# Sum of squares from VectorE to ScalarE, state cast from ScalarE to VectorE, in an 8-core scan and feed-forward layer

## The chip, the cores and the metric

The program runs on the 8 cores of one Trainium2 chip. Each core takes half of one of four sequences; no core waits for another. The metric is the device time of the slowest core in microseconds (us). Before the change it is 3581.18 us, the median of three runs (3579.0 to 3582.77).

## The reference

```python
xn = layernorm(x)                                   # x: 4 x 4096 x 2048, f32
xp = xn @ W_in.T
dt = softplus(xp @ W_dt.T + b_dt)                   # 32 heads
a  = exp(-exp(log_A) * dt)                          # per head and channel
ys[t] = a[t] * ys[t-1] + xp[t]                      # along the sequence
attn = ys @ W_out.T
ffn  = ((silu(xn @ w_gate * s_gate) * (xn @ w_up * s_up)) @ w_down) * s_down
out  = x + attn + ffn
```

`w_gate`, `w_up` and `w_down` are int8, with 8192 inner columns.

## The kernel before, in words

A core works on 2048 output rows and on 256 rows ahead of them, from which the scan takes its start. That makes 18 tiles of 128 rows of `x`. Semaphores are placed by hand; each engine runs its instructions in the order in which the program text emits them.

**Preamble (`emit_wc_step`, 16 steps).** The product of `W_dt` and `W_in` is built: a load of `winN` through GpSimd's queue, 16 small matmuls into `psdtl`, and a copy out by ScalarE (L231). Between these steps the normalization of the first ten tiles is started and of eight of them ended.

**Normalization of a tile.** `emit_ln_front` issues the load of the tile `xtb` on ScalarE's queue (L253) and lets VectorE wait for it; VectorE forms the sum (L259), the sum of squares (L260) and four results of one column (L264 to L271). `emit_ln_back` of that tile comes one to three fronts later: ScalarE makes the scale and the shift (L281 to L287) and the normalized tile `xnb` (L291); SyncE writes it to `xn_scr` (L297). There are three `xtb`, so three loads can be under way. The front of tile i waits for the normalized tile i-3.

**Transposes (`emit_tr`, five chunks).** SyncE waits for all writes of `xn_scr` that were issued, and then issues 16 transposing loads into `xnT` (L314). `emit_dtl` makes the step sizes from a chunk: matmuls L327, ScalarE's softplus (L334 to L343), VectorE's sum and split.

**Two passes over 16 column blocks (`emit_m1_et`).** The first pass covers chunks 0 and 1, the second chunks 2 to 4. A block has two or three small products that spread the step size over channels (L399, L402), ScalarE's exponential `ab` (L407), 32 or 48 matmuls of 512 or 256 columns into `ps_xp` (L421), ScalarE's copy `xpsb` (L436), VectorE's scan into `ysb` (L448) and, for the block before, the cast to bf16 `ybfb` (L467) which GpSimd's queue writes out (L476). The fronts of tiles 10 to 17 stand in blocks 0 to 7 of the first pass, the backs of tiles 8 to 17 in blocks 0 to 9. Chunks 2, 3 and 4 are transposed after blocks 4, 8 and 10; their step sizes are made after blocks 5, 9 and 11.

**The rest** is the gate and up products (L609), and then the down and output products (L720, L726), which follow from about 581 us to the end.

Of the kernel before, what the change touches and what calls it, by code (L numbers as in the profile page):

```python
# [13 lines left out]
AF = mybir.ActivationFunctionType  # L14
ALU = mybir.AluOpType
# [59 lines left out]
def build_nc():  # L75
# [22 lines left out]
    SY, VE, AC, TE, GP = nc.sync, nc.vector, nc.scalar, nc.tensor, nc.gpsimd  # L98

    with contextlib.ExitStack() as top:  # L100
        E = top.enter_context

        r_dx = Ring(top, nc, "r_dx", 3)
# [5 lines left out]
        r_dys = Ring(top, nc, "r_dys", 2)  # L109
# [13 lines left out]
        c_xn = Ct(top, nc, "c_xn")  # L123
# [7 lines left out]
        c_scan = Ct(top, nc, "c_scan")  # L131
# [8 lines left out]
        e_act = Ct(top, nc, "e_act")  # L140
# [10 lines left out]
        stats = E(nc.sbuf_tensor("stats", [P, 48], F32))  # L151
# [3 lines left out]
        def vchain(inst):  # L155
            VE.wait_ge(e_dve.h, e_dve.inc(inst))

        def achain(inst):
            AC.wait_ge(e_act.h, e_act.inc(inst))
# [7 lines left out]
        xt_b = [AE(nc.sbuf_tensor(f"xtb{i}", [P, DM], F32)) for i in range(3)]  # L167
        xn_b = [AE(nc.sbuf_tensor(f"xnb{i}", [P, DM], BF16)) for i in range(3)]
        xsq_s = AE(nc.sbuf_tensor("xsq_s", [P, DM], BF16))
# [9 lines left out]
        ys_b = [AE(nc.sbuf_tensor(f"ysb{i}", [P, 1280], F32)) for i in range(2)]  # L179
        ybf_b = [AE(nc.sbuf_tensor(f"ybfb{i}", [P, 1280], BF16)) for i in range(2)]  # L180
# [11 lines left out]
                  for i in range(2)]  # L192
# [6 lines left out]
                               in_=wdtT3[:, :, :].rearrange("t p c -> p t c")))  # L199
        s_dwc.inc(GP.dma_start(out=sel_sb[0:32, :],  # L200
                               in_=sel_in[:, :, :].rearrange("t p c -> p t c")))
# [43 lines left out]
        def emit_ln_front():  # L245
            i = tile_state["i"]
            tile_state["i"] += 1
            kb = i % 3
            row0 = i * P
            if i >= 3:  # L250
                AC.wait_ge(c_xn.h, i - 2)
            r_dx.refill(AC, kb)
            r_dx.inc(AC.dma_start(out=xt_b[kb][:, :],  # L253
                                  in_=x_full[row0:row0 + P, :]), kb)
            cb = 12 * (i % 3)
            r_dx.wait(VE, kb)
            if i >= 3:
                VE.wait_ge(c_xn.h, i - 2)
            vchain(VE.reduce_sum(out=stats[:, cb:cb + 1], in_=xt_b[kb][:, :], axis=AX))  # L259
            vchain(VE.scalar_tensor_tensor(out=xsq_s[:, :], in0=xt_b[kb][:, :],  # L260
                                           scalar=1.0, in1=xt_b[kb][:, :],
                                           op0=ALU.mult, op1=ALU.mult,
                                           accum_out=stats[:, cb + 1:cb + 2]))
            vchain(VE.tensor_scalar_mul(out=stats[:, cb + 2:cb + 3],  # L264
                                        in0=stats[:, cb:cb + 1], scalar1=-INV_D))
            vchain(VE.tensor_scalar_mul(out=stats[:, cb + 3:cb + 4],
                                        in0=stats[:, cb + 1:cb + 2], scalar1=INV_D))
            vchain(VE.tensor_mul(out=stats[:, cb + 4:cb + 5],
                                 in0=stats[:, cb + 2:cb + 3],
                                 in1=stats[:, cb + 2:cb + 3]))  # L270
            inst = VE.tensor_sub(out=stats[:, cb + 5:cb + 6],  # L271
                                 in0=stats[:, cb + 3:cb + 4],
                                 in1=stats[:, cb + 4:cb + 5])
            c_lnv.inc(inst)
# [99 lines left out]
        def emit_m1_et(p, et):  # L374
# [66 lines left out]
            if gi >= 1:  # L441
                emit_cast_spill(p if gi != NE else 0, gi - 1)
# [16 lines left out]
        def emit_cast_spill(p_of, gi2):  # L459
            k2 = gi2 % 2  # L460
            pln = PASS_LEN[0] if gi2 < NE else PASS_LEN[1]
            p2 = 0 if gi2 < NE else 1
            et2 = gi2 % NE
            AC.wait_ge(c_scan.h, gi2 + 1)
            if gi2 >= 2:
                AC.wait_ge(r_dys.h[k2], r_dys.cnt[k2])
            inst = AC.activation(out=ybf_b[k2][:, 0:pln], in_=ys_b[k2][:, 0:pln],  # L467
                                 func=AF.Copy)
            c_ybf.inc(inst)
            GP.wait_ge(c_ybf.h, c_ybf.n)  # L470
            if p2 == 0:
                tt0, nblk, col0 = 0, 6, WU
            else:
                tt0, nblk, col0 = 6, 10, 0
            r_dys.refill(GP, k2)
            r_dys.inc(GP.dma_start(out=ys_scr[tt0:tt0 + nblk, :, et2, :]  # L476
                                   .rearrange("t p c -> p t c"),
                                   in_=ybf_b[k2][:, col0:col0 + nblk * P]
                                   .rearrange("p (t c) -> p t c", c=P)), k2)
# [3 lines left out]
        for r in range(ND):  # L483
            emit_wc_step(r)
            if r in hb:
                emit_ln_back(hb[r])
            if r in hf:
                emit_ln_front()
            if r == 10:
                emit_tr(0)  # L490
# [8 lines left out]
        for et in range(NE):  # L499
            emit_m1_et(0, et)  # L500
            if et in bk:
                emit_ln_back(bk[et])
            if et in fr:
                emit_ln_front()
            if et == 4:
                emit_tr(2)
            elif et == 5:
                emit_dtl(2)
            elif et == 8:
                emit_tr(3)  # L510
            elif et == 9:
                emit_dtl(3)
            elif et == 10:
                emit_tr(4)
            elif et == 11:
                emit_dtl(4)
        for et in range(NE):
            emit_m1_et(1, et)
        emit_cast_spill(1, 2 * NE - 1)

        n_pexp_all = c_pexp.n
# [43 lines left out]
        def di_loads(j):  # L565
            ks = j % 3
            if j >= 3:
# [9 lines left out]
                               in_=sd_in[0:1, 0:QW].broadcast_to([P, QW])), 0)  # L577
        for j in range(NJ):
            kb = j % 3
# [21 lines left out]
            for gu, (ps, wsb, rng) in enumerate(((ps_g, wg_b, r_dwg),  # L601
                                                 (ps_u, wub_b, r_dwu))):
                rng.wait(TE, kb)
                for ch in range(4):
# [3 lines left out]
                    for dt in range(ND):  # L608
                        inst = TE.matmul(ps[:, cols], wsb[kb][:, dt * P:(dt + 1) * P],  # L609
                                         xnT[:, dt * T + WU + ch * 512:  # L610
                                             dt * T + WU + ch * 512 + 512],
                                         start=(dt == 0), stop=(dt == ND - 1))
                    c_pegu.inc(inst)
            for gu in range(2):
                for ch in range(4):
# [4 lines left out]
                    if gu == 0:  # L620
                        inst = AC.activation(out=g_b[kf2][:, cols], in_=ps_g[:, cols],  # L621
                                             func=AF.Silu, scale=sg_c[:, j:j + 1])
                    else:
                        inst = AC.activation(out=u_b[kf2][:, cols], in_=ps_u[:, cols],  # L624
                                             func=AF.Identity, scale=su_c[:, j:j + 1])
                    c_ev.inc(inst)
            for ch in range(4):
                VE.wait_ge(c_ev.h, 8 * j + 4 + ch + 1)
                if j >= 2:
# [3 lines left out]
                                      in1=u_b[kf2][:, cols]))  # L633
# [3 lines left out]
                                  in_=f_b[kf2][:, :].rearrange("p (t c) -> p t c", c=P)),  # L637
# [37 lines left out]
        for q in range(NQ):  # L675
            kq = q % 2
            if q + 1 < NQ:
                if q + 1 >= 2:
# [3 lines left out]
                                       in_=sd_in[0:1, (q + 1) * QW:(q + 2) * QW]  # L682
# [14 lines left out]
            for tt in range(NTT):  # L697
# [6 lines left out]
                if tt == 2 and q + 1 < NQ:  # L704
# [4 lines left out]
                                     in_=woutT5[q + 1, :, :, :]), (q + 1) % 2)  # L709
# [9 lines left out]
                for dt in range(ND):  # L719
                    inst = TE.matmul(ps_o[ko][:, :], yt_b[kf][:, dt * P:(dt + 1) * P],  # L720
                                     wo_sb[q % 2][:, dt * QW:(dt + 1) * QW],
                                     start=(dt == 0), stop=False)
                for jt in range(NJ):
                    if tt == 0 and jt % GJ == 0:
                        TE.wait_ge(c_wds.h, NG * q + jt // GJ + 1)
                    inst = TE.matmul(ps_o[ko][:, :], ft_b[kf][:, jt * P:(jt + 1) * P],  # L726
                                     wdq_sb[:, jt * QW:(jt + 1) * QW],
                                     start=False, stop=(jt == NJ - 1))
# [3 lines left out]
                if qt >= 4:  # L732
                    VE.wait_ge(r_dout.h[ko], r_dout.cnt[ko])
                c_add.inc(VE.tensor_add(out=ob_b[ko][:, :], in0=ps_o[ko][:, :],  # L734
                                        in1=xs_b[kf][:, :]))
# [4 lines left out]
                                        in_=ob_b[ko][:, :]), ko)  # L740
# [84 lines left out]
```

## Time and profile before

| what | value |
|---|---|
| median of 3 runs | 3581.18 us |
| the profiled execution's own time | 3583.25 us |
| its span, from the first to the last instruction of the slowest core | 3581.7 us |
| spans of the eight cores | 3567.2 to 3581.7 us |
| TensorE busy | 3218.2 us, 90% |
| VectorE busy | 480.7 us, 13% |
| ScalarE busy | 537.0 us, 15% |
| mean granted TensorE clock, slowest core | 0.967 |

```profile
PE   0255997999999999999999999969989997997999
DVE  3253221000000000000000012200022004003000
ACT  2134332111111111111111111100000000000000
PEclk9778998999999999999999999989999998999999
DMA  9575443112111221122111222266565557556443
```

Each digit is the busy share of one of 40 equal slices of the span (89.5 us each) in tenths; PEclk is the granted TensorE clock in tenths of full speed, DMA the mean share of the core's 16 DMA engines. TensorE is full from the sixth slice on. The instructions that the change touches all run in the first seven slices, where TensorE is not yet full. The profiled time and the span differ by 1.55 us, which lie around the instructions.

### The profile page before, as it was taken

The page shows a single profiled execution, that of the slowest core. Times are in us where ns is not written, and L with a number is a line of the kernel's source. Part 1 is how long each engine was busy: PE and PEld are TensorE (multiplying, and loading weights), DVE is VectorE, ACT ScalarE, POOL GpSimd, SP SyncE. Part 2 cuts the span into 40 slices and gives each one's busy share as a digit, 9 for nine tenths or more (in the row PEclk, how much of TensorE's full clock was granted, in tenths as well). Part 3 has the DMA queues.
Part 4 walks back from the last instruction along what each step waited for, and adds up shares of the span by engine and source line. Part 5 has one row for each costly group of instructions (what it writes and reads, how often), then busy time and mean ns, then how long its engine had stood idle before and what let it go on. Part 6 is the DMA issues. An engine that isn't in the chain of part 4 may idle for free.

```text
span 3581.7 us, 36582 instructions; the slowest of 8 cores (3567.2 to 3581.7 us)
## 1 busy us (share of the span) xinstructions
PE 3218.2 (90%) x14792; PEld 1460.0 (41%) x15088; DVE 480.7 (13%) x544; ACT 537.0 (15%) x772; POOL 222.9 (6%) x318
## 2 busy tenths in 40 slices
PE   0255997999999999999999999969989997997999
PEld 0022443444444444444444444434433443443444
DVE  3253221000000000000000012200022004003000
ACT  2134332111111111111111111100000000000000
POOL 1000111001000100010001000100000000000000
PEclk9778998999999999999999999989999998999999
DMA  9575443112111221122111222266565557556443
GB/s 206 120 176 123 78 80 92 53 53 66 58 53 54 61 63 54 53 58 66 53 54 56 68 65 89 77 162 212 188 238 180 184 190 238 178 186 226 176 176 115
DMA packets 126757, 419.02 MB, mean 117 GB/s; under 512 B 51248, under 2 KB 51264, under 8 KB 111488
## 3 DMA queue, kind: packets, MB, share of 16 engines
q0 software_dynamic: 44544, 176.52, 19.3%
q1 hardware_dynamic: 79456, 221.28, 18.1%
q10 hardware_dynamic: 2592, 18.88, 1.7%
q8 instruction: 122, 2.00, 0.2%
q14 instruction: 43, 0.35, 0.0%
HBM read 322.38 MB, written 68.16 MB: 109 GB/s over the span
## 4 chain that ended last, share of the span: by engine, by line
PE 85%; DMA 7%; SPq 4%; DVE 2%; issue 2%; ACT 1%; POOL 0%; ACTq 0%; DVEq 0%; POOLq 0%
PE ps_g L609 25%; PE ps_u L609 25%; PE pso L726 24%; PE pso L720 6%; PE ps_xp L421 5%; SPq L314 3%; DMA wdq_sb<-wd 2%; DMA xtb<-x_full 1%; DMA xn_scr<-xnb 1%; DVE wdq_sb L548 1%; DMA ftb<-f_scr 1%; PE psdtl L327 0%; DMA winNb<-winN 0%; DVE xsq_s L260 0%; DVE stats L259 0%
## 5 line engine op out<-in xcount | busy, mean ns | idle before, releaser
L726 PE MATMUL pso<-wdq_sb,ftb 128*128 128x512 bf16 x4006 | 913.4, 385 | 69.5 <-DVE wdq_sb L548 64.3
L609 PE MATMUL ps_g<-xnT,wgb 128*128 128x512 bf16 x4015 | 891.8, 380 | 23.4 <-DMA wgb<-wg 19.2
L609 PE MATMUL ps_u<-xnT,wub 128*128 128x512 bf16 x4013 | 889.6, 379 | 4.4
L726 PEld LDWEIGHTS pso<-wdq_sb,ftb 128*128 128x128 bf16 x4096 | 403.1, 99 | 568.7 <-issue 99.5
L609 PEld LDWEIGHTS ps_g<-xnT,wgb 128*128 128x128 bf16 x4096 | 400.6, 98 | 504.5 <-issue 22.1
L609 PEld LDWEIGHTS ps_u<-xnT,wub 128*128 128x128 bf16 x4096 | 401.4, 98 | 482.6
L632 DVE TENSOR_TENSOR fb<-gb,ub 128x512 bf16<-128x512 bf16 x256 | 108.8, 425 | 1566.5 <-ACT ub L624 1566.5
L624 ACT ACTIVATE ub<-ps_u,su_c 128x512 bf16<-128x512 f32 x256 | 175.9, 687 | 707.0 <-PE ps_u L609 707.0
L621 ACT ACTIVATE gb<-ps_g,sg_c 128x512 bf16<-128x512 f32 x256 | 175.9, 687 | 705.3 <-PE ps_g L609 705.3
L720 PE MATMUL pso<-wo_sb,ytb 128*128 128x512 bf16 x1011 | 234.7, 384 | 29.2 <-DMA ftb<-f_scr 28.4
L421 PE MATMUL ps_xp<-xnT,winTb 128*128 128x512 bf16 (+1 forms) x1251 | 256.8, 363 | 2.9 <-issue 2.0
L734 DVE TENSOR_TENSOR obb<-pso,xsb 128x512 f32<-128x512 f32 x64 | 44.2, 691 | 1053.2 <-PE pso L726 1053.2
L421 PEld LDWEIGHTS ps_xp<-xnT,winTb 128*128 128x128 bf16 x1280 | 124.0, 99 | 138.5 <-issue 22.1
L636 POOL DMA_DIRECT2D f_scr<-fb x64 | 75.8, 1185 | 1632.3 <-DVE fb L632 1581.2
L720 PEld LDWEIGHTS pso<-wo_sb,ytb 128*128 128x128 bf16 x1024 | 101.3, 99 | 153.4 <-issue 35.9
L548 DVE TENSOR_TENSOR wdq_sb<-wdq_sb,sdqb 128x4096 bf16<-128x4096 bf16 x32 | 140.2, 4421 | 99.0 <-DMA wdq_sb<-wd 99.0
L327 PE MATMUL psdtl<-xnT,wc_sb 128*32 128x512 bf16 (+1 forms) x80 | 25.5, 497 | 131.6 <-DMA xnT<-xn_scr 99.3
L226 PE MATMUL psdtl<-wdtT_s,winNb 128*128 128x32 bf16 x256 | 9.4, 188 | 87.3 <-DMA winNb<-winN 85.2
L327 PEld LDWEIGHTS psdtl<-xnT,wc_sb 128*32 128x32 bf16 x80 | 9.9, 128 | 146.8 <-issue 143.6
L542 POOL DMA_DIRECT2D wdq_sb<-wd x32 | 17.2, 536 | 777.4 <-PE pso L726 776.4
L448 DVE TENSOR_TENSOR_SCAN ysb<-ab,state_s,xpsb 128x1280 f32<-128x1280 f32 x16 | 46.1, 2884 | 120.5 <-ACT xpsb L436 120.5
L259 DVE TENSOR_REDUCE stats<-xtb 128x1 f32<-128x2048 f32 x18 | 41.1, 2286 | 97.1 <-DMA xtb<-x_full 96.9
(57 smaller groups left out, 510.3 us busy)
## 6 DMA issues: line engine op xcount, KB each, us to landing
ftb<-f_scr SPq DMA_DIRECT2D x64, 2048.0 KB, 8.8
ytb<-ys_scr SPq DMA_DIRECT2D x64, 512.0 KB, 9.7
wgb<-wg POOLq DMA_DIRECT2D x64, 512.0 KB, 5.4
wub<-wu POOLq DMA_DIRECT2D x64, 512.0 KB, 6.1
f_scr<-fb POOLq DMA_DIRECT2D x64, 512.0 KB, 5.3
wdq_sb<-wd POOLq DMA_DIRECT2D x32, 1024.0 KB, 15.9
xtb<-x_full ACTq DMA_DIRECT2D x18, 1024.0 KB, 11.3
winTb<-winT POOLq DMA_DIRECT2D x32, 512.0 KB, 6.4
```

Source lines behind the costliest of these rows:

```text
L314: r_dtr.inc(SY.dma_start(out=xnT[:, dt * T + off: dt * T + off + ln], in_=xn_scr[off:off + ln, dt * P:(dt + 1) * P], transpose=True), kc)
L421: inst = TE.matmul(ps_xp6[:, bank * 512: bank * 512 + ln], winT_b[kw][:, dt * P:(dt + 1) * P], xnT[:, dt * T + off: dt * T + off + ln], st ...
L448: inst = VE.tensor_tensor_scan(out=ys_b[k2][:, 0:pln], data0=a_b[k2][:, 0:pln], data1=xps_b[k2][:, 0:pln], initial=init, op0=ALU.mult, op1 ...
L548: c_wds.inc(VE.tensor_tensor(out=wv, in0=wv, in1=sdq_b[q % 2][:, :].unsqueeze(1) .broadcast_to([P, GJ, QW]), op=ALU.mult))
L609: inst = TE.matmul(ps[:, cols], wsb[kb][:, dt * P:(dt + 1) * P], xnT[:, dt * T + WU + ch * 512: dt * T + WU + ch * 512 + 512], start=(dt = ...
L621: inst = AC.activation(out=g_b[kf2][:, cols], in_=ps_g[:, cols], func=AF.Silu, scale=sg_c[:, j:j + 1])
L624: inst = AC.activation(out=u_b[kf2][:, cols], in_=ps_u[:, cols], func=AF.Identity, scale=su_c[:, j:j + 1])
L632: c_f.inc(VE.tensor_mul(out=f_b[kf2][:, cols], in0=g_b[kf2][:, cols], in1=u_b[kf2][:, cols]))
L636: r_df.inc(GP.dma_start(out=f_scr[:, :, j, :].rearrange("t p c -> p t c"), in_=f_b[kf2][:, :].rearrange("p (t c) -> p t c", c=P)), kf2)
L720: inst = TE.matmul(ps_o[ko][:, :], yt_b[kf][:, dt * P:(dt + 1) * P], wo_sb[q % 2][:, dt * QW:(dt + 1) * QW], start=(dt == 0), stop=False)
L726: inst = TE.matmul(ps_o[ko][:, :], ft_b[kf][:, jt * P:(jt + 1) * P], wdq_sb[:, jt * QW:(jt + 1) * QW], start=False, stop=(jt == NJ - 1))
L734: c_add.inc(VE.tensor_add(out=ob_b[ko][:, :], in0=ps_o[ko][:, :], in1=xs_b[kf][:, :]))
```

## The change

Two pieces of work change engines. In `emit_ln_front`, ScalarE makes the sum of squares as an activation (`Square` with an accumulated output) in place of VectorE. It waits for the tile's load right behind the instruction that issues that load, and the following instruction waits for the activation. VectorE keeps the sum and waits for ScalarE's result before the four small operations. In `emit_cast_spill`, VectorE casts `ysb` to `ybfb` in place of ScalarE, and takes over its two waits.

```diff
@@ emit_ln_front
             r_dx.inc(AC.dma_start(out=xt_b[kb][:, :],
                                   in_=x_full[row0:row0 + P, :]), kb)
             cb = 12 * (i % 3)
+            r_dx.wait(AC, kb)
+            if i >= 3:
+                AC.wait_ge(c_xn.h, i - 2)
+            achain(AC.activation(out=xsq_s[:, :], in_=xt_b[kb][:, :], func=AF.Square,
+                                 accum_out=stats[:, cb + 1:cb + 2]))
+            sq_done = e_act.n
             r_dx.wait(VE, kb)
             if i >= 3:
                 VE.wait_ge(c_xn.h, i - 2)
             vchain(VE.reduce_sum(out=stats[:, cb:cb + 1], in_=xt_b[kb][:, :], axis=AX))
-            vchain(VE.scalar_tensor_tensor(out=xsq_s[:, :], in0=xt_b[kb][:, :],
-                                           scalar=1.0, in1=xt_b[kb][:, :],
-                                           op0=ALU.mult, op1=ALU.mult,
-                                           accum_out=stats[:, cb + 1:cb + 2]))
+            VE.wait_ge(e_act.h, sq_done)
@@ emit_cast_spill
-            AC.wait_ge(c_scan.h, gi2 + 1)
+            VE.wait_ge(c_scan.h, gi2 + 1)
             if gi2 >= 2:
-                AC.wait_ge(r_dys.h[k2], r_dys.cnt[k2])
-            inst = AC.activation(out=ybf_b[k2][:, 0:pln], in_=ys_b[k2][:, 0:pln],
-                                 func=AF.Copy)
+                VE.wait_ge(r_dys.h[k2], r_dys.cnt[k2])
+            inst = VE.tensor_copy(out=ybf_b[k2][:, 0:pln], in_=ys_b[k2][:, 0:pln])
             c_ybf.inc(inst)
```

ScalarE in the preamble, from the first load of `x` on. The copies out of `psdtl` are those of preamble steps 1, 2 and 3; the rows `stats` and `xnb` are the back of tile 0. Before:

```order
L253 DMA xtb<-x_full 128x2048
L231 ACTIVATE wc_sb<-psdtl 128x32 x2
L253 DMA xtb<-x_full 128x2048
L231 ACTIVATE wc_sb<-psdtl 128x32
L281 ACTIVATE stats<-stats,eps_c 128x1
L284 ACTIVATE stats<-stats 128x1
L287 ACTIVATE stats<-stats 128x1
L291 ACTIVATE xnb<-xtb,stats 128x2048
```

After; a line of the kernel below L253 has a number that is larger by three:

```order
L253 DMA xtb<-x_full 128x2048
L259 ACTIVATE xsq_s,stats<-xtb 128x2048
L231 ACTIVATE wc_sb<-psdtl 128x32 x2
L253 DMA xtb<-x_full 128x2048
L259 ACTIVATE xsq_s,stats<-xtb 128x2048
L231 ACTIVATE wc_sb<-psdtl 128x32
L284 ACTIVATE stats<-stats,eps_c 128x1
L287 ACTIVATE stats<-stats 128x1
L290 ACTIVATE stats<-stats 128x1
L294 ACTIVATE xnb<-xtb,stats 128x2048
```

An activation that reads the tile stands between one load and the next, and ahead of the copies of the preamble.

ScalarE in blocks 1 and 2 of the first pass, from the exponentials of block 1 on. Before:

```order
L407 ACTIVATE ab<-ps_xp,negA_s 128x512 x2
L436 ACTIVATE xpsb<-ps_xp 128x1024
L467 ACTIVATE ybfb<-ysb 128x1024
L281 ACTIVATE stats<-stats,eps_c 128x1
L284 ACTIVATE stats<-stats 128x1
L287 ACTIVATE stats<-stats 128x1
L291 ACTIVATE xnb<-xtb,stats 128x2048
L253 DMA xtb<-x_full 128x2048
L407 ACTIVATE ab<-ps_xp,negA_s 128x512 x2
```

After:

```order
L410 ACTIVATE ab<-ps_xp,negA_s 128x512 x2
L439 ACTIVATE xpsb<-ps_xp 128x1024
L284 ACTIVATE stats<-stats,eps_c 128x1
L287 ACTIVATE stats<-stats 128x1
L290 ACTIVATE stats<-stats 128x1
L294 ACTIVATE xnb<-xtb,stats 128x2048
L253 DMA xtb<-x_full 128x2048
L259 ACTIVATE xsq_s,stats<-xtb 128x2048
L410 ACTIVATE ab<-ps_xp,negA_s 128x512 x2
```

The cast is gone, and the activation on the tile stands between its load and the exponentials of the next block.

VectorE at the same place, from the scan of block 0 to that of block 1. Before:

```order
L448 SCALAR_TENSOR_TENSOR ysb<-ab,xpsb 128x1024
L456 COPY state_s<-ysb 128x1
L259 TENSOR_REDUCE stats<-xtb 128x1
L260 SCALAR_TENSOR_TENSOR xsq_s,stats<-xtb 128x2048
L264 TENSOR_SCALAR stats<-stats 128x1
L266 TENSOR_SCALAR stats<-stats 128x1
L268 TENSOR_TENSOR stats<-stats 128x1
L271 TENSOR_TENSOR stats<-stats 128x1
L448 SCALAR_TENSOR_TENSOR ysb<-ab,xpsb 128x1024
```

After:

```order
L451 SCALAR_TENSOR_TENSOR ysb<-ab,xpsb 128x1024
L459 COPY state_s<-ysb 128x1
L265 TENSOR_REDUCE stats<-xtb 128x1
L267 TENSOR_SCALAR stats<-stats 128x1
L269 TENSOR_SCALAR stats<-stats 128x1
L271 TENSOR_TENSOR stats<-stats 128x1
L274 TENSOR_TENSOR stats<-stats 128x1
L470 CAST ybfb<-ysb 128x1024
L451 SCALAR_TENSOR_TENSOR ysb<-ab,xpsb 128x1024
```

The 2048-column product is gone from VectorE, and the cast of block 0 stands behind the small operations of the tile.

## Rows read from the trace of the kernel before

**Rows 1.** Busy time by stage: stretch (us from the start), its length, engines.

```profile
core 0: us, PE busy (x) PEld busy (x) DVE busy (x) ACT busy (x) POOL busy (x), PEclk, DMA share, GB/s
...
172.00:359.00 187.00, 110.97 (x457) 45.37 (x468) 74.85 (x87) 71.61 (x97) 15.81 (x23) 0.78 0.61 143
359.00:563.00 204.00, 197.14 (x1004) 96.13 (x1021) 54.14 (x26) 75.18 (x100) 27.12 (x36) 0.98 0.41 75
563.00:3582.00 3019.00, 2889.26 (x13045) 1306.42 (x13312) 296.12 (x353) 356.46 (x516) 165.61 (x230) 0.98 0.36 115
```

**Rows 2.** The chain of waits up to 700 us: start, length (us), what.

```profile
37.44 2.31 DVE xsq_s L260 x2
...
65.34 13.37 DMA xn_scr<-xnb
...
186.12 9.59 DMA xtb<-x_full
...
278.93 1.05 ACT ybfb L467
...
281.39 7.85 DMA xtb<-x_full
```

**Rows 3.** Timeline of the first 30 us: start, length, engine, line, operation, [idle before <- ended by].

```profile
16.79 0.38 ACTq L253 DMA_DIRECT2D xtb<-x_full  x1
...
23.57 0.20 ACT L231 ACTIVATE wc_sb<-psdtl 128x32 bf16<-128x32 f32 x1 [4.32 <-PE psdtl L226]
23.59 0.33 ACTq L253 DMA_DIRECT2D xtb<-x_full  x1
...
28.96 2.29 DVE L259 TENSOR_REDUCE stats<-xtb 128x1 f32<-128x2048 f32 x1 [17.81 <-DMA xtb<-x_full]
```

**Rows 4.** SyncE's queue: the transposes of chunk 0 and the writes behind them.

```profile
78.88 44.43 SPq L314 DMA_TRANSPOSE xnT<-xn_scr  x16
123.47 5.75 SPq L297 DMA_DIRECT2D xn_scr<-xnb  x4
```

**Rows 5.** Timeline around the back of tile 7 and the load of tile 9.

```profile
126.67 2.09 ACT L291 ACTIVATE xnb<-xtb,stats 128x2048 bf16<-128x2048 f32 x1 [26.52 <-DMA xn_scr<-xnb]
126.88 0.33 ACTq L253 DMA_DIRECT2D xtb<-x_full  x1
...
135.84 2.29 DVE L259 TENSOR_REDUCE stats<-xtb 128x1 f32<-128x2048 f32 x1 [24.92 <-DMA xtb<-x_full]
```

**Rows 6.** ScalarE in the first pass: block 0, and the backs of tiles 12, 14, 16.

```profile
183.96 1.02 ACT L436 ACTIVATE xpsb<-ps_xp 128x1024 f32<-128x1024 f32 x1 [8.90 <-PE ps_xp L421]
184.88 0.28 ACT L281 ACTIVATE stats<-stats,eps_c 128x1 f32<-128x1 f32 x1
...
186.00 2.09 ACT L291 ACTIVATE xnb<-xtb,stats 128x2048 bf16<-128x2048 f32 x1
186.12 0.33 ACTq L253 DMA_DIRECT2D xtb<-x_full  x1
188.00 1.25 ACT L407 ACTIVATE ab<-ps_xp,negA_s 128x512 f32<-128x512 f32 x2
...
225.71 2.09 ACT L291 ACTIVATE xnb<-xtb,stats 128x2048 bf16<-128x2048 f32 x1
...
270.03 0.68 ACT L334 ACTIVATE z_s<-psdtl,bdt_c 32x512 f32<-32x512 f32 x1 [30.95 <-PE psdtl L327]
...
281.26 2.09 ACT L291 ACTIVATE xnb<-xtb,stats 128x2048 bf16<-128x2048 f32 x1
...
300.08 2.10 ACT L291 ACTIVATE xnb<-xtb,stats 128x2048 bf16<-128x2048 f32 x1
```

**Rows 7.** The tile `xtb`: issue to landing of its 18 loads, us.

```profile
DMA to landing us min/median/max: 6.8/11.3/19.8
```

**Rows 8.** VectorE's casts of 512 and of 256 columns.

```profile
142.31 0.42 DVE L349 CAST dthi_s<-dtb 32x512 bf16<-32x512 f32 x1
...
365.41 0.28 DVE L349 CAST dthi_s<-dtb 32x256 bf16<-32x256 f32 x1
```

**Rows 9.** The chain of waits, the last cast ahead of the gate products.

```profile
567.16 1.28 ACT ybfb L467
```

## The prediction

> **What bounds the kernel now.** I read the busy time by stage first. From 563 us on TensorE is busy for 2889 of 3019 us, and nothing there is changed; from 359 to 563 it is busy for 197 of 204 us. Between 172 and 359 us it works for 111 of 187 [rows 1], and before that it hardly works (its busy digits in the table of slices are 0 and 2). So the change acts on the start of the program, and every microsecond by which the work at 359 us comes later or earlier is carried to the end. Then I read the chain of waits up to 359 us. It runs through loads of `x`, VectorE's statistics, the normalized tile, its write to `xn_scr` and SyncE's transposes; TensorE's waits hang on the transposes. In this chain stand five pieces like the 2.31 us of the squares on VectorE and one ScalarE cast of 1.05 us [rows 2]. Last I read ScalarE's own timeline, as the change puts a wait there.
>
> How the chain goes: chunks 0 and 1 are transposed when tiles 3 and 7 are written, chunk 2 when tile 12 is, chunk 3 when tile 16 is. So the start of `xnb` for tiles 7, 12 and 16 (126.67, 225.71, 300.08 us [rows 5, 6]) dates each stage.
>
> **Which resource the change takes.** ScalarE issues the load of a tile, and in the new order must see it land before anything else of its queue goes on: the squares, the copies out of `psdtl`, the back of an earlier tile, the exponentials of the next block, and the issue of the next load. Before, up to three loads were under way. Now there is one, and its whole latency L is on ScalarE's path. That the issue of a load stays behind an unsatisfied wait is in the rows: the second load of `x` needs nothing, and it was issued at 23.59 us, right behind the copy out at 23.57, for which ScalarE had sat idle 4.32 us until TensorE's product [rows 3].
>
> The Trainium skill, in Advanced Engine Details and Errata (Sequencer Loop), speaks the other way: an engine instruction is put in a queue and waits there for its semaphore, while the sequencer reads on. By that rule the next load would be issued during the wait, and the sum below would nearly vanish (the first rival). The trace does not agree: by the rule the second load would have been issued at about 17 us, not at 23.59.
>
> **The length of L.** From issue to landing the rows have: 12.2 us for the first load, with three `winN` loads beside it (16.79 to 28.96) [rows 3]; 9.0 for that of tile 9, late in the preamble (126.88 to 135.84) [rows 5]; 9.59 and 7.85 in the first pass [rows 2]; over all 18 the least is 6.8 and the median 11.3, which has loads queued behind one another [rows 7]. With one load at a time and less traffic I take 10.5 for the preamble (midway between 12.2 and 9.0), 9.5 for blocks 0 to 4 (nearest to 9.59, same neighbours) and 8.7 for blocks 6 to 8 (mean of 9.59 and 7.85).
>
> **Part 1, the preamble.** The squares over 2048 columns are not shown on ScalarE; the nearest row is `xnb` of the same shape, 2.09 us [rows 6], and the VectorE form took 2.31 [rows 2]. I take 2.2 with the wait for its end. Up to the start of `xnb` of tile 7, ScalarE's queue now has: nine loads (tiles 0 to 8), nine squares of 2.2 = 19.8, nine copies out that cannot hide, 0.25 each = 2.3, eight times the three small results ahead of `xnb`, 1.15 each (184.88 to 186.00 [rows 6]) = 9.2, one `xnb` with no load behind it = 2.1, and 1 us for gaps: 34.4. An `xnb` with a load behind it hides beside that load, which is issued 0.12 after its start [rows 6]. Start 16.8, first load 12.2, eight of 10.5 = 84: 16.8 + 12.2 + 84 + 34.4 = 147.4 us, against 126.67. **+20.7.** Bounds: L = 9.0 gives 135.4 (+8.7), L = 12.2 gives 161.0 (+34.3).
>
> What else could be late: tile 7 also waits until tile 4 is written, which stands behind the first 16 transposes on SyncE's queue. `xnb` of tile 3 starts at 16.8 + 12.2 + 4 x 10.5 + 16.8 = 87.8, the last term being five squares with a copy out (2.45 each) and four times 1.15; with 2.1, a write of 13.4 [rows 2] and transposes of 44.4 us [rows 4] that ends at 147.7, plus 3.2: 151 (+24). This is near the same value. The transposes were slow beside the loads and may be shorter when there are fewer, so I keep 147.4.
>
> **Part 2, blocks 0 to 4.** From one `xnb` to the next, ScalarE now needs 0.12 to the load's issue, L, 2.2 for the squares, 1.15 for the exponentials (1.25 less overlap), and 2.04 from `xpsb` to `xnb` (183.96 to 186.00): 5.5 + L [rows 6]. TensorE doesn't hide it: it needs 8 us for a block at full clock and waits for the exponentials. Four cycles from tile 8 to tile 12: 4 x (5.5 + 9.5) = 60.0, against 225.71 - 186.00 = 39.7. **+20.3.** Bounds: L = 6.8 gives +9.5, L = 11.3 gives +27.5. The cast that leaves ScalarE is already in this sum.
>
> **Part 3, blocks 6 to 8.** Fronts 13 to 15 end while ScalarE would wait for chunk 2 anyway: it waited 30.95 us for it [rows 6]. From there on: `xnb` of tile 14 started 11.2 us after `z_s`; without the cast, 10.3. Two cycles more: 10.3 + 2 x (5.5 + 8.7) = 38.7 to tile 16, against 30.05. **+8.7.** Bounds: +4.9 (L = 6.8), +13.9 (L = 11.3).
>
> **Part 4, after 311 us.** No tile is loaded any more. The cast on VectorE has 1280 columns; its price by the two smaller casts is 0.28 us for 256 and 0.14 more for each further 256, so 0.84 [rows 8], against 1.28 on ScalarE [rows 9]. In the second pass it stands beside TensorE's 10 us for a block and costs nothing, with the scan behind it delayed by less than a microsecond in a block with over 7 us free; without that cover it would be 16 x 0.84 = 13. Only the last one is on the chain: **-0.4.** The bound is 0 from above, -1.3 if it were free.
>
> The Trainium skill, in VectorE: DVE Perf Modes (Mode 2x_2P), says that a copy with one source in SBUF runs at two elements a cycle even in f32. By its figures an estimate for 1280 columns is (640 + 8 + 150)/0.96 = 0.83 us; the casts in the trace agree.
>
> **Sum.** 20.7 + 20.3 + 8.7 - 0.4 = 49.3 us. On the profiled execution, 3583.25 + 49.3 = 3632.6. Its own time is 2.07 us above the median of the runs, so for that median 3630.5, rounded to 3631. All bounds low: 8.7 + 9.5 + 4.9 - 1.3 = 21.8, so 3603. All high: 34.3 + 27.5 + 13.9 = 75.7, so 3657.
>
> **The rivals.**
>
> 1. *ScalarE's wait is harmless, the shorter statistics count.* If the next load is issued during the wait, loads stay ahead. Then what goes is five pieces of 2.3 and the cast of 1.05, with 0.4 at the end: 3581 - 13 = 3568. For it: the squares are really on the chain, and two engines work on them at once. Against it: the issue at 23.59 us. It decides at whether the load of tile 1 is issued before that of tile 0 has landed. Chance 4%.
> 2. *A lone load is as fast as the fastest seen.* L = 6.8 throughout: the preamble gives 16.8 + 12.2 + 54.4 + 34.4 = 117.8, so the write of tile 4 decides instead (tile 3 at 73.0, then 2.1 + 13.4 + 44.4 + 3.2 = 136.1, +9.4); then +9.5, +4.9, -0.4: +23.4, or 3605. Against it: 6.8 was reached once, beside idle queues. Chance 10%.
> 3. *Contention stays as it was and the first transposes keep their 44.4 us.* L = 12.2 in the preamble, 11.3 later: +75, or 3656. Against it: one load in place of two or three. Chance 10%.
> 4. *The clock.* From 172 to 359 us the granted clock was 0.78 of full speed [rows 1], as TensorE stood idle between stretches. With 7 of 15 us idle in each block it may stay at the lower of its levels (1.2 GHz) in blocks 0 to 4. 36 matmuls then take about twice their 8 us, 15.4 to 16, so a block is bound by TensorE at 16 in place of 15: 4 us more, and up to 6 for blocks 6 to 8 and those that follow: 3641. Chance 10%.
> 5. *Something hides the delay.* The eight cores differ by 14 us in span, and only the slowest counts; a delay of under 7 us would be unseen. It would need the transposes, not ScalarE, to pace all three stages, and the chain shows that they start from the written tile. Chance 2%.
>
> The forecast itself has 64%. This kernel's runs differ so little that 0.2% (7 us) is what can be told from no change. Faster: 4% (rival 1). Same: 3% (rival 5, and the low end of rival 2). Slower: 93%. The range 3602 to 3657 takes in both bounds of L and leaves out rivals 1 and 5 and the tails.
>
> **What would show it.** In the new profile the load of tile 1 is issued at about 31 us, after the squares of tile 0, and from issue to landing the loads no longer queue: median about 10. `xnb` of tile 7 starts near 147, the five `xnb` of blocks 0 to 4 stand 15 us apart, tile 16 is near 350, and the last stage keeps its length of about 3018 us. Waits of ScalarE for `xtb`, none before, should come to some 170 us. I would be wrong if loads are issued during a wait, if the first transposes shrink far below 44 us and still tile 7 is early, or if the later stages change their length.

## The result, and the profile after

| | before | after |
|---|---|---|
| median | 3581.98 us (10 runs) | 3611.25 us (9 runs) |
| ratio of after to before, with its 95% interval | | 1.0074 (1.0061 to 1.0087) |
| profiled execution | 3583.25 us | 3610.24 us |
| spans of the eight cores | 3567.2 to 3581.7 | 3581.0 to 3608.7 |

The change makes the kernel slower, by some 26 us by the ratio (29 us between the medians). Forecast were 49 us, and a range of 3602 to 3657 that holds the median. Both kernels have runs far above their medians, from a disturbance of one or both dies that comes with any kernel; all ratios here leave such runs out.

The busy time by stage, core 5, which is the slowest now (columns as in [rows 1]):

```profile
172.00:359.00 187.00, 101.36 (x370) 38.13 (x368) 55.58 (x72) 67.78 (x89) 13.03 (x19) 0.74 0.61 129
389.00:593.00 204.00, 195.57 (x1008) 94.16 (x1006) 72.24 (x47) 54.88 (x81) 28.11 (x37) 0.99 0.39 74
593.00:3608.00 3015.00, 2905.29 (x13312) 1306.47 (x13312) 294.77 (x354) 353.11 (x513) 164.71 (x229) 0.98 0.37 115
```

The last stage takes 3015 us, against 3019 in [rows 1]. It begins 30 us later than on core 0 before. The whole loss lies ahead of it, as forecast. The 30 us from 359 to 389 are not in these rows; they belong to the first pass, which now ends later.

ScalarE's timeline in the preamble answers [rows 3]:

```profile
16.04 0.39 ACTq L253 DMA_DIRECT2D xtb<-x_full  x1
28.15 1.91 ACT L259 ACTIVATE xsq_s<-xtb 128x2048 bf16<-128x2048 f32 x1 [11.93 <-DMA xtb<-x_full]
29.97 0.19 ACT L259 ACTIVATION_READ_ACCUMULATOR xsq_s<-xtb 128x1 f32 x1
30.30 0.28 ACT L231 ACTIVATE wc_sb<-psdtl 128x32 bf16<-128x32 f32 x2
30.40 0.33 ACTq L253 DMA_DIRECT2D xtb<-x_full  x1
```

The second load of `x` is issued at 30.40 us, after the squares, and no longer at 23.59. One load is under way at a time. The squares cost 1.91 + 0.19 us.

One cycle in the first pass answers [rows 6]:

```profile
196.08 2.09 ACT L294 ACTIVATE xnb<-xtb,stats 128x2048 bf16<-128x2048 f32 x1
196.20 0.33 ACTq L253 DMA_DIRECT2D xtb<-x_full  x1
204.09 1.91 ACT L259 ACTIVATE xsq_s<-xtb 128x2048 bf16<-128x2048 f32 x1 [5.92 <-DMA xtb<-x_full]
205.91 0.19 ACT L259 ACTIVATION_READ_ACCUMULATOR xsq_s<-xtb 128x1 f32 x1
206.30 1.27 ACT L410 ACTIVATE ab<-ps_xp,negA_s 128x512 f32<-128x512 f32 x2 [0.20 <-ACT xsq_s L259]
207.46 1.02 ACT L439 ACTIVATE xpsb<-ps_xp 128x1024 f32<-128x1024 f32 x1
...
209.49 2.09 ACT L294 ACTIVATE xnb<-xtb,stats 128x2048 bf16<-128x2048 f32 x1
```

From one `xnb` to the next it is 13.41 us: 7.89 from the issue of the load to its landing (196.20 to 204.09) and 5.52 for the rest. ScalarE sits idle for 5.92 us of it. Over the first 359 us its wait for tiles is the largest of all its waits (in total, times, longest); before there was none, and some 170 us were forecast:

```profile
ACT xsq_s L259 <- DMA xtb<-x_full: 130.1, 18, 15.3
```

The new chain of waits shows the loads of tiles 0 to 8 (start, length), which now follow each other on it:

```profile
16.04 12.03 DMA xtb<-x_full
30.40 9.76 DMA xtb<-x_full
43.66 4.98 DMA xtb<-x_full
52.24 10.46 DMA xtb<-x_full
66.36 5.76 DMA xtb<-x_full
75.74 9.68 DMA xtb<-x_full
87.83 5.27 DMA xtb<-x_full
98.82 10.39 DMA xtb<-x_full
116.03 6.83 DMA xtb<-x_full
```

Issue to landing of all 18 loads (least, median, greatest) was 6.8/11.3/19.8 in [rows 7]:

```profile
DMA to landing us min/median/max: 5.0/8.1/17.1
```

SyncE's queue, against [rows 4]; the second row has the transposes of chunk 2:

```profile
87.92 34.85 SPq L317 DMA_TRANSPOSE xnT<-xn_scr  x16
...
247.88 32.50 SPq L317 DMA_TRANSPOSE xnT<-xn_scr  x16
```

The eight cores differ by up to some 20 us in this part of the program, so the stages are compared by the mean over the eight cores of a profiled run. "Tile 3" and "tile 7" are the starts of their `xnb`, "chunk 0" is the time of its 16 transposes. The columns from "to tile 8" on are differences of starts: of `xnb` of tiles 7, 8, 12, 16, of the third step size `z_s`, and of SyncE's first load of `s_down`, which is issued when the last scan has ended; the last column is that start itself.

| us, mean of 8 cores | tile 3 | chunk 0 | tile 7 | to tile 8 | to tile 12 | to third `z_s` | to tile 16 | to scans' end | scans' end at |
|---|---|---|---|---|---|---|---|---|---|
| before | 64.9 | 43.3 | 127.4 | 56.7 | 38.0 | 43.0 | 29.1 | 267.7 | 561.9 |
| after | 78.9 | 38.3 | 133.7 | 55.1 | 51.7 | 45.3 | 36.1 | 265.1 | 587.1 |
| squares alone | 80.0 | 39.7 | 136.2 | 55.5 | 54.9 | 42.9 | 37.4 | 266.6 | 593.4 |
| cast alone | 66.5 | 44.1 | 130.2 | 57.4 | 39.2 | 42.9 | 26.5 | 271.3 | 567.5 |
| wait alone | 78.0 | 37.6 | 130.3 | 55.9 | 48.4 | 42.6 | 33.8 | 266.1 | 577.1 |
| one tile ahead | 66.1 | 69.7 | 155.4 | 56.9 | 34.2 | 43.2 | 26.0 | 264.3 | 580.0 |
| first pass only | 66.0 | 44.3 | 129.7 | 56.7 | 54.6 | 42.2 | 37.1 | 266.7 | 587.0 |
| preamble only | 79.9 | 39.1 | 134.9 | 55.9 | 37.2 | 42.3 | 28.5 | 268.2 | 567.2 |
| eight banks | 96.8 | 21.9 | 139.5 | 54.3 | 50.6 | 45.2 | 35.6 | 265.8 | 591.0 |
| pass ahead | 65.9 | 44.1 | 129.3 | 57.7 | 34.6 | 44.7 | 26.0 | 266.5 | 558.9 |
| late `winT` | 65.8 | 34.4 | 119.7 | 56.9 | 37.2 | 42.5 | 29.0 | 267.0 | 552.3 |

After stands 25.1 us behind before at the scans' end: +6.3 up to tile 7, -1.6, +13.7, +2.3, +7.0, -2.6.

Each row is one execution of its kernel, and not all were taken on the same chip. How far such a row can be off is seen at "cast alone": it stands 5.5 us behind before at the scans' end, though its ratio below shows no change. So a few microseconds of one stage are no finding by themselves.

### The profile page after: what moved, and what is told of

The parts are those of the page before. It is cut to its first block, busy times and chain, and to the rows that moved or that the text cites. A ratio compares the mean times of both kernels' runs of the same rounds, so it can differ in the third digit from the quotient of the medians.

```text
span 3608.7 us, 36929 instructions; the slowest of 8 cores (3581.0 to 3608.7 us)
## 1 busy us (share of the span) xinstructions
PE 3252.0 (90%) x15088; PEld 1462.7 (41%) x15088; DVE 463.5 (13%) x540; ACT 538.0 (15%) x776; POOL 223.0 (6%) x318
## 4 chain that ended last, share of the span: by engine, by line
PE 85%; DMA 8%; SPq 2%; ACT 2%; issue 1%; DVE 1%; POOL 0%; ACTq 0%; POOLq 0%; DVEq 0%
PE ps_g L611 25%; PE ps_u L611 24%; PE pso L728 24%; PE pso L722 6%; PE ps_xp L424 5%; DMA xtb<-x_full 3%; SPq L317 2%; DMA wdq_sb<-wd 2%; DVE wdq_sb L550 1%; ACT xsq_s L259 1%; DMA xn_scr<-xnb 1%; DMA ftb<-f_scr 1%; PE psdtl L330 0%; ACT ab L410 0%; DMA wgb<-wg 0%
## 5 line engine op out<-in xcount | busy, mean ns | idle before, releaser
L424 PE MATMUL ps_xp<-xnT,winTb 128*128 128x512 bf16 (+1 forms) x1280 | 269.1, 372 | 0.0
L736 DVE TENSOR_TENSOR obb<-pso,xsb 128x512 f32<-128x512 f32 x64 | 44.3, 692 | 1052.5 <-PE pso L728 1052.5
L722 PEld LDWEIGHTS pso<-wo_sb,ytb 128*128 128x128 bf16 x1024 | 101.2, 99 | 152.5 <-issue 34.2
## 6 DMA issues: line engine op xcount, KB each, us to landing
wdq_sb<-wd POOLq DMA_DIRECT2D x32, 1024.0 KB, 15.9
```

What stands on the lines that cost most here:

```text
L424: inst = TE.matmul(ps_xp6[:, bank * 512: bank * 512 + ln], winT_b[kw][:, dt * P:(dt + 1) * P], xnT[:, dt * T + off: dt * T + off + ln], st ...
```

## The experiments

Theory A: ScalarE's wait for the load that it has just issued makes the loss, since the load's latency and ScalarE's work then follow each other. Rivals: B, the cast behind the statistics on VectorE; C, the mere work of the squares on ScalarE; D, the loss lies in the preamble.

**Squares alone.** The change without its second half:

```diff
 # emit_cast_spill, against the changed kernel
-            VE.wait_ge(c_scan.h, gi2 + 1)
+            AC.wait_ge(c_scan.h, gi2 + 1)
             if gi2 >= 2:
-                VE.wait_ge(r_dys.h[k2], r_dys.cnt[k2])
-            inst = VE.tensor_copy(out=ybf_b[k2][:, 0:pln], in_=ys_b[k2][:, 0:pln])
+                AC.wait_ge(r_dys.h[k2], r_dys.cnt[k2])
+            inst = AC.activation(out=ybf_b[k2][:, 0:pln], in_=ys_b[k2][:, 0:pln],
+                                 func=AF.Copy)
```

> The squares on ScalarE, with its wait for the tile, and the cast left on ScalarE as before. Theory A (the wait for the load is the cost): slower than before by as much as the whole change, about 26 us plus one cast of 1.05 us in each cycle of blocks 0 to 8 that is now back in ScalarE's cycle, 4 to 8 us: ratio 1.009 to 1.010. Theory B (the cast's new place on VectorE, behind the tile's statistics, is the cost): near no change, ratio 0.998 to 1.001.

Measured: 1.0100 (1.0084 to 1.0116). As A says; B is out.

**Cast alone.** The other half, put into the kernel before (the same lines the other way round).

> Only the cast on VectorE, the squares stay there as before. Theory A: the cast leaves ScalarE's chain, 0.4 us at the end of the scans and a few times 1 us in blocks 0 to 8, but VectorE's chain of the tile's statistics gets 0.7 us more in each block: 3 us faster to 2 us slower, ratio 0.999 to 1.001. Theory B: slower by some 26 us, ratio 1.007.

Measured: 1.0002 (0.9992 to 1.0012), as A says.

**Wait alone.** The kernel before with one line more:

```diff
             cb = 12 * (i % 3)
+            r_dx.wait(AC, kb)
             r_dx.wait(VE, kb)
```

> The kernel before, with nothing added but ScalarE's wait for the tile right behind the issue of its load; all work stays where it was. Theory A: the wait alone makes the loss. The squares of 2.1 us leave ScalarE's cycle, but VectorE's 2.3 us come back into the chain: ratio 1.005 to 1.010, loads of x at about 8 us from issue to landing, and tile 12 about 50 us behind tile 8. Theory C (it is the 2.1 us of squares on ScalarE in each block, not the wait): ratio within 0.998 to 1.002.

Measured: 1.0036 (1.0022 to 1.0049). The wait alone costs 13 us, half of the loss and less than forecast; C in its pure form is out too. The rest shows in ScalarE's cycle in the first pass, a quarter of the distance from tile 8 to tile 12. In the timelines of all eight cores it falls into two parts that can be read one by one. The time from the issue of a load to ScalarE's next instruction, L, is 7.7 us with the wait alone, 7.4 after and 7.3 with squares and cast (means of 32 loads). What is left of the cycle is 4.4, 5.53 and 6.45 us, in the last two within 0.01 us on every core. So L hardly changes, and each piece of work that is put on ScalarE lengthens the cycle by its own time: the wait has put all of ScalarE's queue in series with the load.

**One tile ahead.** Same work on the same engines, but the statistics of a tile are emitted behind the issue of the next load:

```diff
             r_dx.inc(AC.dma_start(out=xt_b[kb][:, :],
                                   in_=x_full[row0:row0 + P, :]), kb)
+            if i >= 1:
+                emit_stats(i - 1)
+
+        def emit_stats(i):
+            kb = i % 3
             cb = 12 * (i % 3)
             r_dx.wait(AC, kb)
@@ first pass
+            if et == 8:
+                emit_stats(17)
```

> The changed kernel, with the sum and the squares of a tile emitted one front later, behind the issue of the next load: the same work on the same engines, but a load is under way while ScalarE waits. Theory A: the wait shrinks from about 7 us to about 0 to 3 us a tile, the distance of tiles 8 to 12 returns to about 40 us, and most of the loss is gone: ratio 0.997 to 1.002. Theory C: the work is the same, so the loss stays, ratio 1.006 to 1.008.

Measured: 1.0051 (1.0025 to 1.0077), between the two forecasts; the interval reaches into C's. The table splits it. In the first pass A is borne out: tile 12 comes 34.2 us after tile 8 and tile 16 comes 26.0 us after `z_s`, both better than before the change. But the transposes of chunk 0 take 69.7 us. SyncE's queue on the slowest core, and the chain of waits there:

```profile
81.31 78.62 SPq L322 DMA_TRANSPOSE xnT<-xn_scr  x16
```

```profile
85.61 31.54 SPq L322
117.19 14.97 SPq L322
132.20 13.21 SPq L322
```

Three of the 16 issues take 60 us. The loads beside them stand still as well, as ScalarE's timeline shows:

```profile
94.52 0.34 ACTq L253 DMA_DIRECT2D xtb<-x_full  x1
138.49 1.91 ACT L264 ACTIVATE xsq_s<-xtb 128x2048 bf16<-128x2048 f32 x1 [42.00 <-DMA xtb<-x_full]
```

The last number of the next row is GB/s, the one ahead of it the DMA engines' busy share. The share is over 1 and the traffic low: the packets take long and move little. The row behind it is the same stretch on core 0 before the change, with more traffic at a smaller share:

```profile
100.00:110.00 10.00, 0.00 (x0) 0.00 (x0) 0.00 (x0) 0.00 (x0) 0.00 (x0) 1.00 1.56 107
```

```profile
100.00:110.00 10.00, 0.00 (x0) 0.00 (x0) 4.60 (x4) 0.15 (x1) 0.00 (x0) 1.00 1.10 175
```

One core of this run had 42.7 us for the same transposes and ended at 3556.4 us. So the time of chunk 0 is its own term, and a wide one. Why it takes 62 to 79 us on seven cores and not on the eighth was not settled.

**First pass only, preamble only.** The changed statistics for some tiles, the old ones for the others; the cast stays on ScalarE:

```diff
+            if i >= 10:        # first pass only; preamble only: i < 10
+                ...            # ScalarE's wait and squares, VectorE's sum
+            else:
+                ...            # VectorE's sum and squares
```

> The squares on ScalarE, with the wait, only for tiles 10 to 17 (the first pass); tiles 0 to 9 and the cast as before. Theory A (the cost is the wait in the first pass, where one cycle of ScalarE is about 6.4 us plus the load): the preamble as before, tile 7 at 126 to 130 us; tile 12 about 54 us behind tile 8, tile 16 about 37 behind the third step size: 20 to 25 us slower, ratio 1.006 to 1.007. Theory D (the preamble holds most of the loss): within 8 us of before.

Measured: 1.0076 (1.0061 to 1.0091); tile 12 at 54.6, tile 16 at 37.1.

> The squares on ScalarE, with the wait, only for tiles 0 to 9 (the preamble); the rest as before. Theory A: tile 7 some 5 to 9 us later, the first pass as before: ratio 1.001 to 1.003. The sum as predicted in the first place would be 20 us (1.006). Theory D: 20 us or more.

Measured: 1.0015 (1.0005 to 1.0025); tile 7 comes 7.6 us later. D is out: the preamble makes some 5 us of the loss. The two losses at the scans' end, 25.1 and 5.2 us, add up to 30.3, and "squares alone" has 31.5.

**Eight banks.** Why are the loads short in the changed preamble? TensorE could run at most two steps ahead of ScalarE's copies, and a `winN` load is issued only when TensorE has freed its buffer. So ScalarE's wait could also hold back the traffic beside the load (theory E). In the changed kernel the products get eight PSUM banks in turn:

```diff
-            if dt >= 2:
-                TE.wait_ge(c_evwc.h, dt - 1)
+            if dt >= 8:
+                TE.wait_ge(c_evwc.h, dt - 7)
+            pw = ps_dtl[dt % 8] if dt % 8 < 2 else ps_xp[dt % 8 - 2]
...                              # matmuls and ScalarE's copy use pw for ps_dtl[dt % 2]
```

> The changed kernel, with eight PSUM banks instead of two for the products of the preamble, so that the loads of winN are not held back by ScalarE's late copies. Theory E (the loads of x became short because ScalarE's wait also holds back the winN loads beside them): in the preamble the loads of x rise from about 8 to 11 us, tile 7 comes 10 to 20 us later than in the changed kernel. Theory F (a load is short because there are no longer two or three of x at a time): the loads of x stay at 8 us and tile 7 within 4 us of the changed kernel's.

Measured: 1.0099 (1.0078 to 1.0120). Issue to landing of the loads up to 125 us, each on its run's slowest core: before, after, and this run:

```profile
DMA to landing us min/median/max: 11.4/12.9/19.8
```

```profile
DMA to landing us min/median/max: 5.0/9.7/12.0
```

```profile
DMA to landing us min/median/max: 5.1/11.9/14.2
```

Theory E is shown by the loads (the medians of the eight cores lie at 11.4 to 12.4 here, at 7.9 to 9.9 after) and by tile 3, 18 us later. Tile 7 is only 5.8 us later, less than expected: by then the other loads are through, the last loads of `x` are short, and the transposes of chunk 0 take 21.9 us, nearly as little as those of chunk 1 (20.5).

**Pass ahead.** The first pass one tile ahead, the preamble as it was, the cast on VectorE:

```diff
+            if i < 10:
+                emit_stats_ve(i)          # as before the change
+            elif i >= 11:
+                emit_stats_ac(i - 1)      # as after, behind the next load's issue
@@ first pass
+            if et == 8:
+                emit_stats_ac(17)
```

> Tiles 0 to 9 as before on VectorE; tiles 10 to 17 with the squares on ScalarE, one front later behind the next load's issue; the cast on VectorE. Theory A: the preamble as before (tile 7 at 126 to 131 us), tile 12 about 34 us behind tile 8 (38 before), tile 16 about 26 behind the third step size (29 before), so 5 to 8 us faster: ratio 0.998. If the gain of the first pass in the run one tile ahead only came from its later start: ratio 1.000.

Measured: 0.9989 (0.9974 to 1.0004): the stages as A says, 3 us earlier at the scans' end. The interval reaches to no change, so the ratio alone does not tell the two forecasts apart.

**Late `winT`.** The kernel before, with the first three loads of `winT` behind the transposes of chunks 0 and 1:

```diff
+        r_dtr.wait(GP, 0)
+        r_dtr.wait(GP, 1)
         emit_winT_load(0)
```

> The kernel before, with the first three loads of winT held back until chunks 0 and 1 are transposed. Theory G (the transposes of chunk 0 take 43 us in place of 21 because plain loads are under way beside them, three of winT among them): the transposes of chunk 0 shrink by 5 to 10 us, tile 7 comes that much earlier, ratio 0.997 to 0.999. If they are slow for another cause: they stay at 43, ratio 1.000.

Measured: 0.9973 (0.9961 to 0.9985). Theory G is shown for the `winT` loads: chunk 0 goes from 43.3 to 34.4 us and tile 7 from 127.4 to 119.7. That other loads make the rest, down to some 21 us, fits "eight banks" but was not tested by itself. SyncE's queue on the slowest core:

```profile
80.20 36.52 SPq L314 DMA_TRANSPOSE xnT<-xn_scr  x16
```

**Late `winT` and pass ahead.** Both edits together.

> The same hold on winT, with tiles 10 to 17 one front later on ScalarE and the cast on VectorE (the fastest so far). The two gains lie in stages that follow each other and should add: ratio 0.995 to 0.998.

Measured: 0.9948 (0.9931 to 0.9966), the fastest version by its ratio, 19 us below before. By the profiled executions it is 14 us (3568.88 against 3583.25), so the sign is surer than the size. Both gains are there in the table's terms: tile 7 at 120.1 us, tile 12 33.6 behind tile 8, the scans' end at 549.4.

**`winT` held back for chunk 0 only.** The same without `r_dtr.wait(GP, 1)`.

> As the previous one, but winT held back only until chunk 0 is transposed, so its loads run beside the writes and transposes of chunk 1. Theory G: chunk 0 gains the same, chunk 1 loses 0 to 5 us of it: ratio 0.996 to 0.999.

Measured: 0.9957 (0.9925 to 0.9990). From tile 7 to tile 8 it has 63.4 us where the previous one has 57.1. The transposes of chunk 1 are hardly longer (21.1 us against 20.4); the loss lies ahead of them, where the `winT` loads run beside the writes of the last tiles: from `xnb` of tile 7 to the first transpose of chunk 1 it is 15.9 us against 9.7. The intervals of the two ratios overlap.

**Pass ahead, cast on ScalarE.** As "pass ahead", with the cast left where it was.

> Tiles 10 to 17 one front later on ScalarE, the cast left on ScalarE. The cast of 1.05 us is then back in ScalarE's queue in each block. With the load's wait gone the cast's place matters by up to 1 us in each of six cycles, or not at all: ratio 0.999 to 1.001, at most 4 us above the same kernel with the cast on VectorE.

Measured: 0.9992 (0.9978 to 1.0006). The cast's place makes no difference that can be told.

## Why the prediction was right, and where its sizes were off

Direction, path and wait were as forecast; the size forecast was nearly twice the one measured. All three parts came out too large, and Part 1 even fell below its own lower bound of +8.7. The range held because the other two parts stayed within theirs. The one term that was mis-sized in each part is L, the time of a load.

- **The mechanism** was right. The load of tile 1 was expected at about 31 us and came at 30.40; a wait of ScalarE was expected to stand between issue and landing, and it does. Rival 1, by which the next load is issued during the wait, is out with that row. The load of tile 1 has no wait of its own and was issued 14 us after that of tile 0. I had put such a row against a rule of the Trainium skill in Advanced Engine Details and Errata (Sequencer Loop), by which an engine instruction is pushed into a queue and waits for its semaphore. That went too far: the waits of this kernel are statements of their own (`wait_ge`), ahead of the instruction, and the rows do not tell where in the engine such a wait is held. They show that the issue of a load does not pass it.
- **Part 1**, +20.7 forecast, +6.3 measured. The term that was mis-sized is L = 10.5 for eight loads. The chain above has 7.9 on the mean of eight, and 16.0 + 12.0 + 63.1 + 34.4 = 125.5 gives tile 7, measured 126.4 on that core. Over all eight cores the same loads have a mean of 8.7, and 16.8 + 12.2 + 8 x 8.7 + 34.4 = 133.0 gives their mean of 133.7. The 34.4 us of ScalarE's work were right. I had taken L from loads with the old traffic beside them; "eight banks" shows that the new wait thins that traffic. Nor did the transposes of chunk 0 keep 44.4 us: with fewer loads beside them they took 38.3. The second path of the forecast, through these transposes and the write of tile 4, is in fact about as long as the first: on cores 0, 1 and 7 it ended last, as on core 1, where `xnb` of tile 7 still waited 1.19 us for a write:

```profile
126.37 2.09 ACT L294 ACTIVATE xnb<-xtb,stats 128x2048 bf16<-128x2048 f32 x1 [1.19 <-DMA xn_scr<-xnb]
```

- **Part 2**, +20.3 forecast, +13.7 measured: a cycle of 5.5 + 9.5 forecast, 5.5 + 7.4 measured. Here the error is at least in part in the choice of the row: I took L from core 0, the slowest before. Issue to landing from 165 to 345 us on core 0, and then on core 5, both of the kernel before:

```profile
DMA to landing us min/median/max: 6.8/9.4/11.3
```

```profile
DMA to landing us min/median/max: 5.5/7.4/10.3
```

  By this median six cores have 7.4 to 7.8 us before the change; only cores 0 and 6 have more (9.4 and 9.1), and these two also have the longest way from tile 8 to tile 12, 39.7 and 39.8 us against 38.0 as a mean. A cost that is to hold on all cores must not be read from the one.
- **Not in the sum**: -1.6 from tile 7 to tile 8, +2.3 from tile 12 to the third step size and -2.6 behind tile 16. In the middle one the load of tile 15 and the transposes of chunk 2 run beside each other: on core 5 the one took 17.1 us to land and the others 32.5, and as a mean over the cores these transposes went from 23.6 to 27.0. "Wait alone" (42.6) and "squares alone" (42.9) do not have these 2.3 us, and all three are within what one execution can be off, so their cause stays open.
- **Part 3**, +8.7 forecast, +7.0 measured: again L, forecast at 8.7 and measured at 7.5 (mean of two loads on eight cores).
- **Part 4**: 0.84 us for the cast forecast, 0.83 measured, and hidden in the second pass, as forecast. VectorE's timeline, core 5:

```profile
593.83 0.83 DVE L470 CAST ybfb<-ysb 128x1280 bf16<-128x1280 f32 x1 [0.24 <-DVE ysb L451]
```

- **Rivals.** Rival 2 (a lone load is fast) came nearest by its time, 3605, and had 10%. For the first pass its L of 6.8 is nearer to the 7.4 measured than my 9.5. In the preamble its reason is wrong: a lone load with the other traffic still beside it has a median of 11.4 to 12.4 us, as "eight banks" shows. Rival 3 (contention stays) is out by the same loads: they were shorter, and the transposes too. Rival 4: the granted clock from 172 to 359 us did fall, from 0.78 to 0.74, and some blocks ran at about 9 us for 32 matmuls in place of 7; ScalarE's cycle of 13 us covers that in the first pass. The slow block that stands on the chain behind it (8.78 us at 390 us, the first one after the last step sizes) has its like before, so no cost of the clock shows there. The block of the first pass, after, and the one behind the last step sizes, before:

```profile
195.51 8.95 PE L424 MATMUL ps_xp<-xnT,winTb 128*128 128x512 bf16 x32
```

```profile
363.80 8.74 PE L421 MATMUL ps_xp<-xnT,winTb 128*128 128x512 bf16 x31
```

## What to carry to other kernels

Before an operation is moved to an engine that also issues the loads of its operand, ask what stands between the issue and the wait: the same work one tile later in the queue took 28 us less over two stages of the first pass (34.2 + 26.0 against 51.7 + 36.1). The latency of a load is not a constant to be carried over from the old trace; a wait that slows the issuer thins the traffic beside the load, and the price shrinks with it. And when a stage is made faster, look at what its loads will now run beside.

## What the runs showed of the hardware that was not expected

- Sixteen DMA transposes of a 512-row chunk take 20.4 us with little beside them, 43.3 us beside loads of `x`, `winN` and `winT`, 34.4 us when the three `winT` loads are taken away, 21.9 us when all other loads but those of `x` are through, and up to 78.6 us in one arrangement. There the stall sits in a few of the 16 issues, and other loads stall with them (42 us of waiting for one load of 1 MB, at 40 to 107 GB/s of traffic for the core).
- An activation with an accumulated output over 2048 columns took 1.91 us and 0.19 us for reading the accumulator; VectorE's form took 2.29 and 0.08.
